# Attention with rotary queries and keys: projecting a query half and a key half in turn instead of all queries and then all keys

## The chip, the cores and the metric

The kernel runs on one core of a Trainium2 chip. A core has TensorE (PE in the profile, with its weight loads shown as PEld), VectorE (DVE), ScalarE (ACT), GpSimd (POOL) and SyncE (SP), each with its own instruction stream; they are ordered only by semaphores. The metric is the device time of one execution in microseconds, lower is better.

## The reference

A transformer block for 32 batch elements ("batches" below) of 256 tokens and 128 channels, all in float32. Only the attention part is touched:

```
h = layernorm(x) * (1 + ca) + sa
q = rope(rmsnorm(einsum('bim,mhd->bhid', h, wq)))      # 8 heads, D = 128
k = rope(rmsnorm(einsum('bim,mhd->bhid', h, wk)))
v = einsum('bim,mhd->bhid', h, wv)
s = q @ k^T / 128, causal mask, softmax
x = x + ga * einsum('bhid,hdm->bim', softmax(s) @ v, wo)
# then a mixture of experts: top 2 of 8, h = layernorm(x) * (1 + cb) + sb
x = x + gb * experts(h)

def _rope(x):   # even, odd are the halves of the last axis
    return concatenate([even * cos - odd * sin, even * sin + odd * cos])
```

## The kernel before

The first part of the kernel is a software pipeline over batches. One body handles, for body number n, the projections of batch n (stage A), the transposes and the value product of batch n-1 (stage B), scores, exponentials and values of batch n-2 (stage C), the residual of batch n-3 (R), the second normalization of n-4 (N2), the routing of n-5 (RT) and the scatter of rows of n-6 (ST). The second part runs the experts and begins when the first has ended; the change doesn't touch it.

Each engine runs the body in eight steps, h = 0 to 7, and each step holds one head of stage C beside one eighth of stage A. The order of the instructions on each engine is the order in which the code is written; there is no scheduler.

**Stage A.** Queries and keys each have TT = 2 token tiles of 128 tokens and H*D = 1024 columns, worked in halves of 512 columns. That gives eight products of 128x512 per batch, four of queries (steps 0 to 3) and four of keys (steps 4 to 7). Product h is written by TensorE (`split_product`, three matmuls, L1225 in the profile) to the PSUM tile `UN[0]` ("unit" in the profile), which has two banks; product h goes to bank h % 2. ScalarE then squares it for the RMS norm (L753), and VectorE rotates it:

- a key half in two operations: `cosines` (L1073) writes product*cos to `roped`, `sines` (L1085) writes the swapped product*sin to `rope_b`; GpSimd adds the two (`add`, L565, semaphore `add_done`).
- a query half (from batch 1 on) in three: `sines` to `rope_b`, `cosines` in place in PSUM, and the sum of both to `roped` (L1120, semaphore `q_added`). In batch 0 the query halves are done like keys.

TensorE may overwrite a bank when VectorE has ended its last read: for a key that is the sines (`rope_done`), for a query the sum (`q_added`). GpSimd scales the finished queries of the batch before by their RMS factors (`scale_queries`, L574), TensorE transposes the tiles of `roped` (L1312) in steps 0, 1 (keys) and 5, 6 (queries), and ScalarE copies them out of the second PSUM tile `UN[1]` (L770).

**Stage C.** In each step TensorE computes the scores of head h, and then the product of values and probabilities of head h-1 (`values_times_probs`, L1249 to L1252, "pv" in the profile). Head 7 has no step after it, so its product follows that of head 6 at once, at the end of step 7. VectorE adds each head's result into `acc`, one step later than the product and in two halves (`add_head`, L1046; L1042 for head 0). The two "pv" buffers alternate, and the code holds product g until head g-2 has been added in full:

```python
def values_times_probs(b, h):
    g = H * b + h
    wait(pe, "exp_done", 2 * (g + 1))
    wait(pe, "acc_done", TT * (g - 1))
```

**Routing.** From body 5 on VectorE also carries small operations of the router, placed by step: among them the maxima (L976, step 5, which wait for GpSimd's `score`, L640), the copy of rows (L1024, steps 4 and 5) and `one_hot` (L985, step 6, just before the first half of `add_head`).

Of the kernel before, what the change touches and what calls it, by code (L numbers as in the profile page):

```python
# [14 lines left out]
ALU = mybir.AluOpType  # L15
# [4 lines left out]
def adaln_block(nc, x, wq, wk, wv, wo, wr, br, w1, b1, w2, b2, c, wmod, rope_cos, rope_sin, out):  # L20
# [40 lines left out]
    with ctx:  # L61
# [246 lines left out]

        PIECE_FROM, HI_AT, LO_AT = 2, 5, 7
# [146 lines left out]
        def _(pool):  # L456
# [50 lines left out]
            def body(half, parity, live):  # L507
# [53 lines left out]
                def add(h):  # L561

                    u, heads = h // 2, slice(h % 2 * HH * D, (h % 2 + 1) * HH * D)
                    wait(pool, "rope_done", 2 * NU * n + h + 1)
                    pool.tensor_tensor(out=roped[parity][:, u, heads], in0=roped[parity][:, u, heads],  # L565
                                       in1=rope_b[:, u % 2, heads], op=ALU.add)\
                        .then_inc(S["add_done" if h >= HH else "q_added"], 1)
# [36 lines left out]
                if n == 0:  # L604
                    add(0)
# [5 lines left out]
                if n == 0:  # L611
                    for h in range(1, HH):
                        add(h)
# [4 lines left out]
                if ST:  # L618
# [5 lines left out]
                                       op=ALU.mult).then_inc(S["place_k_done"], 1)  # L624
                if B:
                    if A:
                        wait(pool, "q_added", HH * n + 3)
                    scale_queries(1)
                if now:
                    scatter(n - 6, parity, 0, 0)  # L630
                if X:
# [4 lines left out]
                        .then_inc(S["h_ready"], 1)  # L636
                if RT:
# [5 lines left out]
                if A:  # L643
                    add(4)
# [9 lines left out]
                if A:  # L654
                    add(5)
# [6 lines left out]
                if A:  # L662
                    add(6)
# [25 lines left out]
        def _(act):  # L689
# [26 lines left out]
            def body(half, parity, live):  # L716
                n = 2 * half + parity
                _, X, A, B, C, R, N2, RT, ST = live
                for h in range(H):
# [24 lines left out]
                    if A:  # L744

                        w, u = 2 * NU * n + h, h // 2
# [4 lines left out]
                        for j in range(HH):  # L751
                            c = HH * (h % 2) + j
                            nc.scalar.activation(squares[:, c * D:(c + 1) * D], UN[0][:, c * D:(c + 1) * D],  # L753
# [85 lines left out]
        def _(dve):  # L839
# [98 lines left out]
            def body(half, parity, live, heads=H):  # L938
# [121 lines left out]
                for h in range(heads):  # L1060
                    w, u, bank = 2 * NU * n + h, h // 2, h % 2
                    t = u % TT
                    heads = slice(bank * HH * D, (bank + 1) * HH * D)
                    in_place = h < HH and n > 0

                    def cosines():
# [3 lines left out]
                        else:  # L1070
                            wait(dve, "tr_done", NU * (n - 1))
                        turned = UN[0][:, heads] if in_place else roped[parity][:, u, heads]
                        nc.vector.tensor_tensor(  # L1073
                            out=turned.rearrange("p (g c) -> p g c", c=D // 2),
                            in0=UN[0][:, heads].rearrange("p (g c) -> p g c", c=D // 2),
# [3 lines left out]
                    def sines():  # L1079

                        if h < HH:
                            wait(dve, "add_done", HH * (n - 1) + h + 1)
                        elif n == 0:
                            wait(dve, "q_added", h - HH + 1)
# [1100 lines left out]
```

## Time and profile before

| | |
|---|---|
| median of 3 runs | 1124.4 us (1123.93 to 1126.92) |
| profiled execution, its own time | 1132.29 us |
| its span, first to last instruction | 1130.5 us |
| busy, share of the span | PE 90%, ACT 85%, DVE 79%, POOL 70% |
| mean granted TensorE clock | 0.965 |

The execution's own time is 1.8 us above its span. A busy share is an average over the attention part (until about 791 us) and the expert part behind it. Times in the rows further down are microseconds from the start of the span. A timeline row gives start, duration, engine, line, operation, tiles with shapes, how often it repeats, and in brackets the idle time ahead of it with what ended it. VectorE's and ScalarE's next instruction can start some 0.1 us before the row of the one before it ends.

### The profile page before, as it was taken

The page shows a single profiled execution, that of the slowest core. Times are in us where ns is not written, and L with a number is a line of the kernel's source. Part 1 is how long each engine was busy: PE and PEld are TensorE (multiplying, and loading weights), DVE is VectorE, ACT ScalarE, POOL GpSimd, SP SyncE. Part 2 cuts the span into 40 slices and gives each one's busy share as a digit, 9 for nine tenths or more (in the row PEclk, how much of TensorE's full clock was granted, in tenths as well). Part 3 has the DMA queues.
Part 4 walks back from the last instruction along what each step waited for, and adds up shares of the span by engine and source line. Part 5 has one row for each costly group of instructions (what it writes and reads, how often), then busy time and mean ns, then how long its engine had stood idle before and what let it go on. Part 6 is the DMA issues. An engine that isn't in the chain of part 4 may idle for free. (4 is left out here: it accounts for less than half of the span.)

```text
span 1130.5 us, 27394 instructions
## 1 busy us (share of the span) xinstructions
PE 1018.9 (90%) x7294; PEld 780.5 (69%) x7294; DVE 896.2 (79%) x2757; ACT 963.0 (85%) x3517; POOL 785.7 (70%) x1197
## 2 busy tenths in 40 slices
PE   5899999999999999999999999999898779989700
PEld 3588888888888888888888888888554434558600
DVE  5788888889998889888888888886768746767647
ACT  6999999999999999999999999997797748888424
POOL 6655578877787877777777777777356675656654
PEclk9999999999999999999999999999999988999955
DMA  5410000100000100000000000000442322320158
GB/s 151 132 34 13 14 17 26 37 25 23 24 23 27 35 15 13 16 16 15 16 16 16 14 16 15 16 15 18 126 112 92 97 77 65 90 68 26 37 188 271
DMA packets 53849, 57.91 MB, mean 51 GB/s; under 512 B 8108, under 2 KB 42783, under 8 KB 53700
## 3 DMA queue, kind: packets, MB, share of 16 engines
q1 hardware_dynamic: 36612, 35.11, 10.5%
q0 software_dynamic: 8640, 16.87, 4.5%
q10 hardware_dynamic: 8448, 4.20, 1.3%
q8 instruction: 63, 1.03, 0.4%
q14 instruction: 86, 0.70, 0.2%
HBM read 33.08 MB, written 23.97 MB: 50 GB/s over the span
## 5 line engine op out<-in xcount | busy, mean ns | idle before, releaser
L753 ACT ACTIVATE squares<-unit 128x128 f32<-128x128 f32 x1024 | 273.3, 303 | 3.6 <-PE unit L1225 3.4
L565 POOL TENSOR_TENSOR roped<-roped,rope_b 128x512 f32<-128x512 f32 x132 | 175.1, 1327 | 91.7 <-DVE rope_b L1085 89.3
L753 ACT ACTIVATION_READ_ACCUMULATOR squares<-unit 128x1 f32 x1024 | 235.2, 236 | 0.0
L1567 POOL DMA_INDIRECT y_rows<-y_out,place_y x142 | 152.2, 1072 | 94.7 <-DVE y_out L1989 49.4
L1085 DVE TENSOR_TENSOR rope_b<-unit,sin_sb 128x512 f32<-128x512 f32 x256 | 174.4, 681 | 14.6 <-ACT squares L753 12.3
L731 ACT ACTIVATE probs<-scores,rr 128x256 f32<-128x256 f32 x256 | 124.3, 485 | 43.5 <-issue 27.4
L1046 DVE SCALAR_TENSOR_TENSOR acc<-pv,den,acc 128x128 f32<-128x128 f32 x448 | 146.2, 341 | 0.3
L1312 PEld LDWEIGHTS unit<-ident_wr,roped 128*128 128x128 f32 x1024 | 117.9, 141 | 31.6 <-ACT k_t L770 13.0
L1312 PE MATMUL unit<-ident_wr,roped 128*128 128x128 f32 x1024 | 135.2, 275 | 1.6 <-POOL roped L565 1.5
L1975 DVE TENSOR_TENSOR hid_lo<-hidden,hid_hi 128x512 f16<-128x512 f32 (+1 forms) x144 | 92.3, 685 | 54.1 <-ACT hid_hi L1675 34.5
L574 POOL TENSOR_TENSOR roped<-roped,rr 128x1024 f32<-128x1024 f32 x64 | 121.5, 1899 | 13.0 <-DVE roped L1120 12.2
L594 POOL DMA_INDIRECT x_rows<-rows,place x108 | 109.1, 1010 | 22.6 <-issue 19.2
L1665 ACT ACTIVATE hidden<-up,b_t 128x512 f32<-128x512 f32 (+1 forms) x184 | 99.0, 598 | 20.3 <-remote 10.6
L1073 DVE TENSOR_TENSOR roped<-unit,cos_sb 128x512 f32<-128x512 f32 x132 | 89.7, 679 | 25.6 <-ACT squares L753 25.2
L1225 PE MATMUL unit<-wqk_hi,h_hi 128*128 128x512 f16 x256 | 97.9, 382 | 7.3 <-DVE rope_b L1085 4.1
L1249 PE MATMUL pv<-vals,probs 128*128 128x129 f32 x512 | 101.1, 279 | 0.1
L1030 DVE RECIPROCAL den<-pv 128x2 f32<-128x2 f32 x256 | 40.6, 159 | 74.1 <-PE pv L1252 74.0
L1267 PE MATMUL scores<-q_t,k_t 128*128 128x128 f32 x512 | 98.9, 275 | 0.5 <-ACT q_t L770 0.5
L1252 PE MATMUL pv<-vals,probs 128*128 128x129 f32 x512 | 99.0, 275 | 0.0
L1269 PE MATMUL scores<-q_t,k_t 128*128 128x128 f32 x512 | 99.0, 275 | 0.0
L1250 PE MATMUL pv<-vals,probs 128*128 128x129 f32 x512 | 99.0, 275 | 0.0
L1270 PE MATMUL scores<-q_t,k_t 128*128 128x128 f32 x512 | 99.0, 275 | 0.0
(304 smaller groups left out, 3061.3 us busy)
## 6 DMA issues: line engine op xcount, KB each, us to landing
shared<-y_rows SPq DMA_DIRECT2D x16, 512.0 KB, 5.6
x_all<-in_L_attn_x SPq DMA_DIRECT2D x32, 128.0 KB, 2.2
h_late<-in_L_ffn_W SPq DMA_DIRECT2D x16, 256.0 KB
out_x<-hidden ACTq DMA_DIRECT2D x16, 256.0 KB, 3.4
rope_b<-x_rows SPq DMA_DIRECT2D x13, 258.0 KB
tile_x<-x_rows SPq DMA_DIRECT2D x12, 258.0 KB
y_rows<-y_out,place_y POOLq DMA_INDIRECT x142
ga_b<-mod_dram SPq DMA_DIRECT2D x32, 64.0 KB
```

The source lines that it names most:

```text
L565: pool.tensor_tensor(out=roped[parity][:, u, heads], in0=roped[parity][:, u, heads], in1=rope_b[:, u % 2, heads], op=ALU.add)\
L574: pool.tensor_tensor(out=v, in0=v, in1=r, op=ALU.mult).then_inc(S["qs_done"], 1)
L594: pool.indirect_dma_start(out=x_rows, out_offset=bass.IndirectOffsetOnAxis(ap=at, axis=0), in_=rows[k][:, j, t, :], in_offset=None).then_i ...
L731: nc.scalar.activation(probs[:, h % NPR, 0:T], SC[h % 2][:, 0:T], ACT.Exp, scale=r[:, kc:kc + 1]).then_inc(S["exp_done"], 1)
L753: nc.scalar.activation(squares[:, c * D:(c + 1) * D], UN[0][:, c * D:(c + 1) * D], ACT.Square, accum_out=ssq[parity][:, u * H + c:u * H + ...
L1046: ins = nc.vector.scalar_tensor_tensor(out=a[:, t, :], in0=o[:, t, 0:M], scalar=den[:, h % 2, t:t + 1], in1=a[:, t, :], op0=ALU.mult, op1= ...
L1085: nc.vector.tensor_tensor(out=rope_b[:, u % 2, heads].rearrange("p (h s c) -> p h s c", h=HH, s=2), in0=UN[0][:, heads].rearrange("p (h s ...
L1249: nc.tensor.matmul(o[:, 0:D + 1], pr[:, 0:P], v[:, 0, h, 0:D + 1], start=True, stop=True)
L1250: nc.tensor.matmul(o[:, VW:VW + D + 1], pr[:, P:2 * P], v[:, 0, h, 0:D + 1], start=True, stop=False)
L1252: nc.tensor.matmul(o[:, VW:VW + D + 1], pr[:, 2 * P:3 * P], v[:, 1, h, 0:D + 1], start=False, stop=True).then_inc(S["o_done"], 1)
L1312: ins = nc.tensor.transpose(UN[1][:, j * P:(j + 1) * P], roped[other][:, u, j * D:(j + 1) * D], ident[:, :])
L1567: pool.indirect_dma_start(out=y_rows, out_offset=bass.IndirectOffsetOnAxis(ap=place_y[i % (2 * SLOTS)][:, s:s + 1], axis=0), in_=y_out[at] ...
```

## The change

`projection(h)` gives each step a new product: kind = h % 2, half = h // 2 % 2, token tile = h // 4. Steps 0, 2, 4 and 6 hold query halves, steps 1, 3, 5 and 7 key halves. All queries now go to bank 0 and all keys to bank 1 of `UN[0]`. Query halves are summed by VectorE in every batch, batch 0 too. GpSimd's four key additions move in its program: `add(1)` behind the offsets, `add(3)` between the two `scale_queries` (its wait for the third `q_added` is gone), `add(5)` and `add(7)` in the places of the old `add(4)` and `add(7)`; the subtraction that makes `h_lo` now comes ahead of the first scatter. The core of the diff:

```diff
+        def projection(h):
+
+            kind, half, t = h % 2, h // 2 % 2, h // HH
+            return kind, half, t, kind * TT + t
...
-                if n == 0:
-                    for h in range(1, HH):
-                        add(h)
+                if A:
+                    add(1)
                 if rest:
                     scatter(n - 7, other, 1, 1)
                 if B:
...
+                if A:
+                    add(3)
                 if B:
-                    if A:
-                        wait(pool, "q_added", HH * n + 3)
                     scale_queries(1)
-                if now:
-                    scatter(n - 6, parity, 0, 0)
                 if X:
...
+                if now:
+                    scatter(n - 6, parity, 0, 0)
                 if RT:
...
                 if A:
-                    add(4)
+                    add(5)
...
                 for h in range(heads):
-                    w, u, bank = 2 * NU * n + h, h // 2, h % 2
-                    t = u % TT
-                    heads = slice(bank * HH * D, (bank + 1) * HH * D)
-                    in_place = h < HH and n > 0
+                    w = 2 * NU * n + h
+                    bank, half_of, t, u = projection(h)
+                    product = UN[0][:, bank * HH * D:(bank + 1) * HH * D]
+                    heads = slice(half_of * HH * D, (half_of + 1) * HH * D)
+                    in_place = h % 2 == 0
...
-                        wait(pe, "rope_done", w - 1)
-                        was, left = (n, h - 2) if h >= 2 else (n - 1, h - 2 + H)
-                        if was > 0 and left < HH:
-                            wait(pe, "q_added", HH * was + left + 1)
+                        if kind:
+                            wait(pe, "rope_done", w - 1)
+                        else:
+                            wait(pe, "q_added", w // 2)
```

VectorE in steps 4 to 6 of a body with routing. Before, all three steps hold keys (cosines L1073, sines L1085); the rows start behind the last `den` of step 3 and run to the end of step 6, with step 5 left out:

```order
L968 TENSOR_REDUCE e_sum<-e_lg 128x2
L1073 TENSOR_TENSOR roped<-unit,cos_sb 128x512
L971 RECIPROCAL e_rec<-e_sum 128x2
L1046 SCALAR_TENSOR_TENSOR acc<-pv,den,acc 128x128
L1024 COPY rows<-pv 128x2x128
L1046 SCALAR_TENSOR_TENSOR acc<-pv,den,acc 128x128
L1085 TENSOR_TENSOR rope_b<-unit,sin_sb 128x512
...
L1073 TENSOR_TENSOR roped<-unit,cos_sb 128x512
L985 TENSOR_TENSOR one_hot<-iota_e,top_i 128x32
L1046 SCALAR_TENSOR_TENSOR acc<-pv,den,acc 128x128 x2
L1085 TENSOR_TENSOR rope_b<-unit,sin_sb 128x512
```

The same place of the changed kernel, where steps 4 and 6 hold queries (L1120 is the sum; most other lines have moved by one or a few numbers):

```order
L967 TENSOR_REDUCE e_sum<-e_lg 128x2
L1085 TENSOR_TENSOR rope_b<-unit,sin_sb 128x512
L970 RECIPROCAL e_rec<-e_sum 128x2
L1045 SCALAR_TENSOR_TENSOR acc<-pv,den,acc 128x128
L1023 COPY rows<-pv 128x2x128
L1073 TENSOR_TENSOR unit<-unit,cos_sb 128x512
L1045 SCALAR_TENSOR_TENSOR acc<-pv,den,acc 128x128
L1120 TENSOR_TENSOR roped<-unit,rope_b 128x512
...
L984 TENSOR_TENSOR one_hot<-iota_e,top_i 128x32
L1045 SCALAR_TENSOR_TENSOR acc<-pv,den,acc 128x128
L1073 TENSOR_TENSOR unit<-unit,cos_sb 128x512
L1045 SCALAR_TENSOR_TENSOR acc<-pv,den,acc 128x128
```

Steps 4 and 6 each hold one 512-column operation more than before (and steps 1 and 3 one less), and in step 6 a 512-column operation now stands between the two halves of `add_head`.

GpSimd from the offsets (L557) to the score of the router (L640), before:

```order
L557 TENSOR_TENSOR off<-mv,rr 128x2 x2
L594 DMA x_rows<-rows,place 69376x129
L574 TENSOR_TENSOR roped<-roped,rr 128x1024
L622 TENSOR_TENSOR place_k<-one_hot,place_e 128x32
L574 TENSOR_TENSOR roped<-roped,rr 128x1024
L594 DMA x_rows<-rows,place 69376x129
L635 TENSOR_TENSOR h_lo<-h_t,h_hi 128x256
L640 TENSOR_TENSOR score<-e_lg,e_rec 128x16
```

and in the changed kernel:

```order
L562 TENSOR_TENSOR off<-mv,rr 128x2 x2
L571 TENSOR_TENSOR roped<-roped,rope_b 128x512
L599 DMA x_rows<-rows,place 69376x129
L579 TENSOR_TENSOR roped<-roped,rr 128x1024
L624 TENSOR_TENSOR place_k<-one_hot,place_e 128x32
L571 TENSOR_TENSOR roped<-roped,rope_b 128x512
L579 TENSOR_TENSOR roped<-roped,rr 128x1024
L635 TENSOR_TENSOR h_lo<-h_t,h_hi 128x256
L599 DMA x_rows<-rows,place 69376x129
L642 TENSOR_TENSOR score<-e_lg,e_rec 128x16
```

Two key additions (L571) have moved ahead of the score, and the scatter and `h_lo` have changed places.

## Rows read from the trace of the kernel before

**Rows 1.** The page: busy time of the engines.
```profile
PE 1018.9 (90%) x7294; PEld 780.5 (69%) x7294; DVE 896.2 (79%) x2757; ACT 963.0 (85%) x3517; POOL 785.7 (70%) x1197
```

**Rows 2.** Busy time in stretches: PE, PEld, DVE, ACT, POOL, clock, DMA.
```profile
16.80:35.10 18.30, 13.22 (x66) 7.44 (x64) 13.75 (x25) 15.51 (x79) 13.71 (x19) 0.91 0.39 110
53.40:76.50 23.10, 23.10 (x175) 18.99 (x175) 18.54 (x50) 21.52 (x94) 13.32 (x19) 1.00 0.25 66
407.40:431.55 24.15, 24.15 (x185) 19.82 (x183) 21.66 (x74) 23.00 (x98) 19.01 (x32) 1.00 0.05 16
407.65:422.80 15.15, 15.15 (x113) 11.89 (x112) 12.71 (x40) 14.91 (x64) 13.01 (x24) 1.00 0.06 17
790.90:815.00 24.10, 19.31 (x148) 15.25 (x146) 15.70 (x77) 16.50 (x37) 9.86 (x21) 1.00 0.43 124
```

**Rows 3.** Timeline of TensorE, one body's products 0, 6, 7 and its last pv.
```profile
407.40 0.38 PE L1225 MATMUL unit<-wqk_hi,h_hi 128*128 128x512 f16 x1
...
425.44 0.38 PE L1225 MATMUL unit<-wqk_hi,h_hi 128*128 128x512 f16 x1
...
428.41 0.38 PE L1225 MATMUL unit<-wqk_hi,h_hi 128*128 128x512 f16 x1
...
429.50 0.39 PE L1250 MATMUL pv<-vals,probs 128*128 128x129 f32 x2
429.73 0.39 PE L1252 MATMUL pv<-vals,probs 128*128 128x129 f32 x2
430.03 0.46 PE L1249 MATMUL pv<-vals,probs 128*128 128x129 f32 x2
...
431.55 0.38 PE L1225 MATMUL unit<-wqk_hi,h_hi 128*128 128x512 f16 x1
```

**Rows 4.** Timeline of VectorE, steps 3 to 6 of the same body.
```profile
421.46 0.69 DVE L1120 TENSOR_TENSOR roped<-unit,rope_b 128x512 f32<-128x512 f32 x1
422.06 0.17 DVE L1030 RECIPROCAL den<-pv 128x2 f32<-128x2 f32 x1
...
422.85 0.69 DVE L1073 TENSOR_TENSOR roped<-unit,cos_sb 128x512 f32<-128x512 f32 x1 [0.56 <-ACT squares L753]
...
424.37 0.68 DVE L1085 TENSOR_TENSOR rope_b<-unit,sin_sb 128x512 f32<-128x512 f32 x1
...
426.01 0.23 DVE L976 MAX8 top_s<-score 128x8 f32<-128x8 f32 x2
...
427.27 0.68 DVE L1085 TENSOR_TENSOR rope_b<-unit,sin_sb 128x512 f32<-128x512 f32 x1
...
428.07 0.68 DVE L1073 TENSOR_TENSOR roped<-unit,cos_sb 128x512 f32<-128x512 f32 x1
428.66 0.70 DVE L985 TENSOR_TENSOR one_hot<-iota_e,top_i 128x32 f32<-128x32 f32 x1
429.29 0.60 DVE L1046 SCALAR_TENSOR_TENSOR acc<-pv,den,acc 128x128 f32<-128x128 f32 x2
```

**Rows 5.** Timeline of ScalarE: the exponentials of head 0 of the next body.
```profile
431.80 0.47 ACT L731 ACTIVATE probs<-scores,rr 128x256 f32<-128x256 f32 x1 [0.91 <-issue]
```

**Rows 6.** Timeline of GpSimd, steps 3 to 6 of the same body.
```profile
419.12 1.90 POOL L574 TENSOR_TENSOR roped<-roped,rr 128x1024 f32<-128x1024 f32 x1
421.17 1.01 POOL L594 DMA_INDIRECT x_rows<-rows,place  x1 [0.15 <-issue]
423.21 0.67 POOL L635 TENSOR_TENSOR h_lo<-h_t,h_hi 128x256 f16<-128x256 f32 x1 [1.03 <-ACT h_hi L760]
423.85 0.20 POOL L640 TENSOR_TENSOR score<-e_lg,e_rec 128x16 f32<-128x16 f32 x1
...
428.03 1.28 POOL L565 TENSOR_TENSOR roped<-roped,rope_b 128x512 f32<-128x512 f32 x1 [0.23 <-DVE rope_b L1085]
```

**Rows 7.** All instructions of the line of one_hot: ns min/median/max, first and last start.
```profile
L985 DVE TENSOR_TENSOR one_hot<-iota_e,top_i x28: 172/694/703, 138.9 to 786.9; 128x32 f32<-128x32 f32 x28
```

More of the change, by code:

```diff
@@ L603, in body @@
                     roots()
-                if n == 0:
-                    add(0)
                 if R:
@@ L751, in body @@
                         for j in range(HH):
-                            c = HH * (h % 2) + j
-                            nc.scalar.activation(squares[:, c * D:(c + 1) * D], UN[0][:, c * D:(c + 1) * D],
+                            c, at = HH * half_of + j, (HH * bank + j) * D
+                            nc.scalar.activation(squares[:, at:at + D], UN[0][:, at:at + D],
                                                  ACT.Square, accum_out=ssq[parity][:, u * H + c:u * H + c + 1])\
@@ L1071, in cosines @@
                             wait(dve, "tr_done", NU * (n - 1))
-                        turned = UN[0][:, heads] if in_place else roped[parity][:, u, heads]
+                        turned = product if in_place else roped[parity][:, u, heads]
                         nc.vector.tensor_tensor(
                             out=turned.rearrange("p (g c) -> p g c", c=D // 2),
-                            in0=UN[0][:, heads].rearrange("p (g c) -> p g c", c=D // 2),
+                            in0=product.rearrange("p (g c) -> p g c", c=D // 2),
                             in1=cos_sb[:, t:t + 1, :].to_broadcast([P, 2 * HH, D // 2]),
@@ L1079, in sines @@
                     def sines():
[L1081 to L1084, printed above, removed]
+                        if in_place:
+                            wait(dve, "add_done", HH * (n - 1) + h // 2 + 1)
+                        else:
+                            wait(dve, "q_added", HH * n + h // 2 + 1)
                         nc.vector.tensor_tensor(
-                            out=rope_b[:, u % 2, heads].rearrange("p (h s c) -> p h s c", h=HH, s=2),
-                            in0=UN[0][:, heads].rearrange("p (h s c) -> p h s c", h=HH, s=2)[:, :, ::-1, :],
+                            out=rope_b[:, t, heads].rearrange("p (h s c) -> p h s c", h=HH, s=2),
+                            in0=product.rearrange("p (h s c) -> p h s c", h=HH, s=2)[:, :, ::-1, :],
                             in1=sin_sb[:, t, :].rearrange("p (o s c) -> p o s c", o=1, s=2)
@@ L1119, in body @@
                         wait(dve, "tr_done", NU * (n - 1))
-                        nc.vector.tensor_tensor(out=roped[parity][:, u, heads], in0=UN[0][:, heads],
-                                                in1=rope_b[:, u % 2, heads], op=ALU.add).then_inc(S["q_added"], 1)
+                        nc.vector.tensor_tensor(out=roped[parity][:, u, heads], in0=product,
+                                                in1=rope_b[:, t, heads], op=ALU.add).then_inc(S["q_added"], 1)
                     elif A:
```

27 lines of the change are left out of this document (12 added, 15 removed).

## The prediction

> **What bounds the kernel now.** The page's busy times [rows 1] name TensorE first, but they mix two parts of the program, so I went to the stretches. One body of the attention part, from its product 0 to that of the next body, lasts 24.15 us [rows 3], and the busy times of that stretch [rows 2] show TensorE busy in all of it, ScalarE 23.00, VectorE 21.66 and GpSimd 19.01 us. So TensorE sets the pace, ScalarE is 1.15 us from doing so, and VectorE 2.5 us.
>
> Busy matmuls overlap, so that alone doesn't show that TensorE never waits. The timeline does: its matmuls start at steady distances of about 0.22 us for a pair of 128x129 passes, 429.50 to 429.73 for one. The next start would be due at 429.95, and it comes at 430.03 [rows 3]. That start is the values product of head 7. It has waited for VectorE: by the code it needs both halves of head 5 added, and that pair of additions runs from 429.29 to 429.89 [rows 4]. From the end of the additions to the matmul are 0.14 us. So the addition of head 5 in step 6 is already on the path, with about nothing to spare; a stall of some 0.08 us per body is there now. What comes late there makes everything late, since TensorE is full and can't catch up.
>
> The Trainium skill bears on that last sentence (Perfetto Trace Analysis, "Identifying the Most-Contended Engine"): matmul busy time is no measure of TensorE's headroom, the weight loads' busy share is a better one. Weight loads are busy 19.82 of the 24.15 us here, and by that rule a body would have up to 4.3 us in which to absorb a stall, so that this change might cost nothing. The timeline speaks against it, since the starts leave no gap; I keep it as one reason behind the rival of no change.
>
> The second view is VectorE's timeline. Step 4 begins when ScalarE has squared product 4: the cosines start at 422.85 after 0.56 us of idle [rows 4]. From there to the additions of head 5 VectorE has no idle time. That is a chain of 7.04 us (422.85 to 429.89) of VectorE alone. What anchors its start is ScalarE: from the exponentials of head 0 to the squares of product 4, 407.65 to 422.80, it is busy 14.91 of 15.15 us [rows 2]. In front of the exponentials of head 0 ScalarE idles 0.91 us, because it waits for TensorE's scores, which come behind that values product [rows 5]. So there is a loop: ScalarE to step 4, VectorE through steps 4 to 6, TensorE's product of head 7 and its scores, and ScalarE again. It takes the 24.15 us of a body.
>
> **The change part by part.**
> A 512-column operation of VectorE takes 0.68 us as a row and 0.60 us from its start to the next one's (421.46 to 422.06, and 428.07 to 428.66 is 0.59) [rows 4]. The change adds none and removes none from body 1 on; it moves the query sum out of steps 1 and 3 into steps 4 and 6.
>
> - *Steps 1 and 3 get 0.60 us shorter each.* Worth nothing: step 4 can't start before the squares of product 4, and VectorE already idles 0.56 us there.
> - *Step 4 gets the sum: +0.60 us* on the chain.
> - *Step 6 is a query step.* Its sines take the place of the cosines, but its own cosines now stand between the two halves of the addition of head 5: +0.60 us ahead of the second half. (Its sum comes behind, and falls on the next waits, which have slack: product 0 of the next body needs it.)
>
> That makes the addition of head 5 end at 429.89 + 1.20 = 431.09, and the values product of head 7 start at 431.23 instead of 430.03: **+1.20 us**.
>
> - *The maxima of step 5.* They need GpSimd's score, which now has two key additions ahead of it. The second, add(3), can't start before the sines of step 3. Step 3 loses its sum, which ended at 421.46 + 0.69 = 422.15 [rows 4], so its last operation, now the sines, ends near 421.55. Then 1.28 (add, rows 6) to 422.91, 1.90 (scaling) to 424.81, 0.64 (h_lo, start to start) to 425.45, the scatter 0.15 + 1.01 to 426.61, and the score 0.20 to 426.83. VectorE would reach the maxima at 426.01 + 0.60 = 426.61 and gets to them near 426.9: **+0.3 us**. If the scatter is quicker to issue or overlaps this is 0; if GpSimd needs 0.2 us more somewhere it is 0.5.
> - *one_hot.* It works on 32 columns and takes 0.694 us in the median, and 0.172 us in its shortest case, the last one [rows 7], at 786.9, where no key addition runs beside it any more. In the body shown it ends with GpSimd's key addition (428.03 + 1.28 = 429.31; 428.66 + 0.70 = 429.36) [rows 4, 6]. The key addition of step 5 still starts just behind the sines of step 5, so I take the same 0.70 us: **+0**. If the two no longer met, the chain would be up to 0.5 us shorter: **-0.5**.
>
> The last point agrees with a rule of the Trainium skill (SBUF — State Buffer, "Who interferes with whom"): an operation of VectorE with both inputs in SBUF contends with a GpSimd instruction that reads SBUF, and one of the two is blocked until the other ends. If that rule held for any pair at any time, each query sum that now runs beside a key addition would be a candidate too; but its first input is in PSUM, so the rule adds nothing for it.
>
> - *Products 6 and 7.* Product 6 needs the sum of step 4. From the first rotation of step 4 to the second are 1.52 us (422.85 to 424.37), then 0.60 and the sum's own 0.68: 425.65; with the latency of 0.14 it is 425.79, against the product's start at 425.44 [rows 3]: 0.35 us late. Product 7 needs the sines of step 5, which ended at 427.27 + 0.68 = 427.95 [rows 4]: 427.95 + 0.60 + 0.3 + 0.14 = 428.99 against 428.41 [rows 3], 0.58 late. Both lie inside the later +1.5 and are not added to it.
> - *GpSimd.* It does four key additions per body as before and has 5.1 us to spare [rows 2]. Behind add(3) in its queue stand the scaling, h_lo, the scatter and the score. The scaling ends at 424.8 by the working above, and the transposes of that tile come behind product 6, so after 426: hidden. h_lo is for the next body. Only the score is waited for in time.
> - *Batch 0 and 1.* VectorE takes four sums of 0.68 from GpSimd in batch 0; VectorE is busy 13.75 of 18.30 us there [rows 2]: within 1 us either way.
>
> **The sum.** 1.2 + 0.3 = 1.5 us per body. It needs routing on VectorE (the small operations and one_hot) together with projections, which is bodies 5 to 31, 27 of them: one_hot runs 28 times [rows 7], the last without projections. In bodies 2 to 4, without routing, VectorE is busy 18.54 of 23.10 us [rows 2]; there the chain is about 1.5 us shorter (one_hot and the small ones) and the extra 1.2 is absorbed. 27 x 1.5 = 40.5; body 31 has less on ScalarE and gives a little back, so **+40 us**. The profiled execution would go from 1132.3 to about 1172; the median of the runs is 7.9 us below that execution, nothing that the change touches explains this, so I add to the median: 1124.4 + 40 = **1164 us**.
>
> **The rivals.**
> 1. *The stall is smaller* (the score comes in time, or one_hot no longer meets a GpSimd addition, or both): 1.2 - 0.5 = 0.7 us per body, (product 7 alone would still be 0.3 late): 27 x 0.3 to 27 x 0.8 = 8 to 22 us, 1132 to 1146.
> 2. *Nothing changes.* TensorE would have to absorb the stall, by starting later work closer together. The spacing speaks against it. 1124.
> 3. *Faster.* Place: the same values product. If the first half's lighter steps let VectorE run ahead, so that head 5 is added before 429.81, the 0.08 us wait there goes, 2.2 us in 27 bodies, and the same lead could give 1 to 3 us in bodies 0 and 1, where TensorE is busy only 13.22 of 18.30 us [rows 2]: 3 to 5 us, 1119 to 1121. It decides itself at the start of step 4: VectorE would have to start it 1.2 us before the squares of product 4 are done, and the trace has it waiting for exactly these.
> 4. *More than that*: GpSimd becomes the bound. Its order now holds scaling behind add(3). If its operations stretch by over 1 us, the score, the query transposes and the values product all slip: 2 to 3 us per body, 1178 to 1205.
> 5. *The clock.* A wait of 1.5 us per 25 could cost TensorE its clock. Where it was busy only 19.31 of 24.10 us the granted clock was 1.00, the 2.4 GHz level [rows 2]; it was 0.91 only in the first stretch. I give it no share of its own.
>
> **How the numbers follow.** The forecast (1.0 to 1.9 us per body, 1151 to 1176) gets 0.72, rival 1 0.12, rival 2 0.04, rival 3 0.06, rival 4 0.06. A measurement here can tell about 0.3%, 3.4 us, from no change. Slower by more: 0.72 + 0.12 + 0.06 = 0.90, less 0.01 for a rival 1 at its edge: 0.89; the same 0.05, faster 0.06. The range of 8 in 10 takes the forecast and the upper end of rival 1, 1144 to 1178.
>
> **What the profile after would show.** Bodies 5 to 31 last about 25.65 us instead of 24.15, bodies 2 to 4 about 23.15 as now. TensorE gets a gap of over 1 us before the values product of head 7, released by VectorE's additions (L1045), and short ones before products 6 and 7. VectorE's steps 4 to 6 run without idle time except before the maxima, where 0.3 us for the score stand. ScalarE's idle time before the exponentials of head 0 grows from 0.9 to about 2.4 us. It would be wrong if bodies last 24.2 us, if the gap lies before products 0 to 5, or if VectorE waits for GpSimd by 1 us or more.

## The result, and the profile after

| | before | changed |
|---|---|---|
| median (lowest to highest) of 4 runs | 1125.66 us (1123.93 to 1128.32) | 1177.39 us (1175.49 to 1178.36) |
| span of the profiled execution | 1130.5 us | 1173.7 us |
| mean granted TensorE clock | 0.965 | 0.966 |

The changed kernel takes 1.0455 times as long (95% interval 1.0428 to 1.0482), 51.7 us more. The two profiled spans differ by only 43.2 us, because the execution profiled before was 6.6 us above the median of before while the one after is 1.9 us below its own. What differs is the expert part behind the attention part, which the change doesn't touch; so the bodies below are the better measure.

The first line of the page after shows that every engine is now busy for a smaller share than in [rows 1]:

```profile
PE 1032.1 (88%) x7294; PEld 781.2 (67%) x7294; DVE 903.2 (77%) x2761; ACT 968.2 (82%) x3517; POOL 777.8 (66%) x1193
```

To see where in the program the time went I measured each body from the logarithm that ScalarE computes at its start to the next one. There are 35, so one per body, up to the end of the attention part. These are distances worked out from the timelines, in us:

| bodies | before | changed | difference, summed |
|---|---|---|---|
| 0 and 1 | 18.26, 18.28 | 21.06, 19.84 | +4.36 |
| 2 to 4 | 23.16, 23.15, 23.37 | 23.38, 23.36, 23.38 | +0.44 |
| 5 to 31 | 24.08, then 24.15, the last 22.80 | 25.26, 25.79, then 26.10 to body 18, 25.71 from 19, the last 23.86 | +46.29 |
| start-up and last bodies | | | -0.02 |
| all | | | +51.07 |

So the loss is where it was forecast, in bodies 5 to 31, but there are two kinds of body, 26.1 and 25.7 us. The windows of one body of each kind stand for the 24.15 us window of [rows 2] (columns: length, then busy time of PE, PEld, DVE, ACT, POOL with their numbers of instructions, granted clock, DMA share and rate):

```profile
408.45:434.56 26.11, 24.59 (x185) 19.82 (x184) 21.84 (x74) 23.21 (x98) 18.96 (x31) 1.00 0.08 24
589.70:615.40 25.70, 24.44 (x184) 19.69 (x183) 20.88 (x73) 22.87 (x97) 18.57 (x31) 1.00 0.05 15
```

VectorE, ScalarE and GpSimd have no more work than before, within some 0.2 us. TensorE has gaps; its row of busy time (24.59 us) overlaps and can hide them. Its timeline of the first of these bodies answers to [rows 3]. It shows products 6 and 7, the end of the values product of head 6, that of head 7, and product 0 of the next body:

```profile
426.77 0.39 PE L1225 MATMUL unit<-wqk_hi,h_hi 128*128 128x512 f16 x1
...
430.44 0.39 PE L1225 MATMUL unit<-wqk_hi,h_hi 128*128 128x512 f16 x1 [0.52 <-DVE rope_b L1085]
...
431.76 0.39 PE L1252 MATMUL pv<-vals,probs 128*128 128x129 f32 x2
433.04 0.46 PE L1249 MATMUL pv<-vals,probs 128*128 128x129 f32 x2 [0.90 <-DVE acc L1045]
...
434.56 0.38 PE L1225 MATMUL unit<-wqk_hi,h_hi 128*128 128x512 f16 x1
```

Product 7 waits 0.52 us for the sines of step 5, and the values product of head 7 waits 0.90 us for the addition of head 5. It was forecast that the gap at the values product would be over 1 us and the one at product 7 short; the loss is spread more evenly over both. VectorE's timeline of the same body, against [rows 4]:

```profile
421.25 0.19 DVE L1013 TENSOR_REDUCE place<-place_k 128x4 int32<-128x32 f32 x1 [0.44 <-POOL place_k L624]
...
422.47 0.68 DVE L1085 TENSOR_TENSOR rope_b<-unit,sin_sb 128x512 f32<-128x512 f32 x1
...
423.92 0.69 DVE L1085 TENSOR_TENSOR rope_b<-unit,sin_sb 128x512 f32<-128x512 f32 x1 [0.62 <-ACT squares L752]
...
426.03 0.68 DVE L1120 TENSOR_TENSOR roped<-unit,rope_b 128x512 f32<-128x512 f32 x1
...
428.43 0.24 DVE L975 MAX8 top_s<-score 128x8 f32<-128x8 f32 x2 [0.67 <-POOL score L642]
...
431.09 0.69 DVE L984 TENSOR_TENSOR one_hot<-iota_e,top_i 128x32 f32<-128x32 f32 x1
431.70 0.34 DVE L1045 SCALAR_TENSOR_TENSOR acc<-pv,den,acc 128x128 f32<-128x128 f32 x1
431.96 0.68 DVE L1073 TENSOR_TENSOR unit<-unit,cos_sb 128x512 f32<-128x512 f32 x1
432.56 0.33 DVE L1045 SCALAR_TENSOR_TENSOR acc<-pv,den,acc 128x128 f32<-128x128 f32 x1
...
435.58 0.67 DVE L1128 SCALAR_TENSOR_TENSOR w_lo<-h_late,w_hi 128x512 f16<-128x512 f32 x1
```

The sum (L1120) of step 4 and the cosines between the halves of head 5's addition stand where the prediction put them. The wait of 0.67 us for the score is more than the 0.3 forecast, and there is a wait that was not forecast at all, 0.44 us for GpSimd's `place_k` in step 3. In bodies from 19 on the first shrinks and the second is gone, but for 0.16 us in body 23:

```profile
635.02 0.24 DVE L975 MAX8 top_s<-score 128x8 f32<-128x8 f32 x2 [0.27 <-POOL score L642]
```

The view of waits over the stretch from 150 to 780 us (total, times, longest) shows that split. VectorE waits for the score in every body of the stretch, 24 times, and for `place_k` 13 times, in bodies 7 to 18 and in body 23:

```profile
PE pv L1249 <- DVE acc L1045: 21.5, 24, 0.9
...
DVE top_s L975 <- POOL score L642: 11.5, 24, 0.7
...
DVE place L1013 <- POOL place_k L624: 5.4, 13, 0.4
```

### The profile page after: what moved, and what is told of

It is laid out like the page before. It is cut to its first block and busy times, and to the rows that moved or that the text cites. A ratio compares the mean times of both kernels' runs of the same rounds, so it can differ in the third digit from the quotient of the medians.

```text
span 1173.7 us, 27269 instructions
## 1 busy us (share of the span) xinstructions
PE 1032.1 (88%) x7294; PEld 781.2 (67%) x7294; DVE 903.2 (77%) x2761; ACT 968.2 (82%) x3517; POOL 777.8 (66%) x1193
## 5 line engine op out<-in xcount | busy, mean ns | idle before, releaser
L571 POOL TENSOR_TENSOR roped<-roped,rope_b 128x512 f32<-128x512 f32 x128 | 169.9, 1327 | 201.4 <-DVE rope_b L1085 201.4
L1085 DVE TENSOR_TENSOR rope_b<-unit,sin_sb 128x512 f32<-128x512 f32 x256 | 174.0, 680 | 42.2 <-ACT squares L752 40.0
L1249 PE MATMUL pv<-vals,probs 128*128 128x129 f32 x512 | 101.4, 280 | 24.3 <-DVE acc L1045 24.1
L1249 PEld LDWEIGHTS pv<-vals,probs 128*128 128x128 f32 x512 | 80.3, 190 | 34.5 <-issue 28.8
L1252 PE MATMUL pv<-vals,probs 128*128 128x129 f32 x512 | 99.0, 275 | 0.0
```

Source lines behind the costliest of these rows:

```text
L1085: nc.vector.tensor_tensor(out=rope_b[:, t, heads].rearrange("p (h s c) -> p h s c", h=HH, s=2), in0=product.rearrange("p (h s c) -> p h s ...
L1249: nc.tensor.matmul(o[:, 0:D + 1], pr[:, 0:P], v[:, 0, h, 0:D + 1], start=True, stop=True)
```

## The experiments

The ten kernels of the experiments ran in three series: a_add_first, a_onehot_late, a_score_early and b_half_late on one chip and a_first_and_score, a_all_three, a_key_first and b_onehot_late on another, on both of which the kernel before takes 1094.7 us, and b_sum0 and a_key_first_onehot on a third, where it takes 1136.5 us. No trace of the kernel before was taken there. The expert part, which none of the edits touches, lasts, counted from the last logarithm, 298.8 us in the trace of b_half_late, 340.1 in that of b_sum0 and 339.6 in that of before, while bodies that an edit doesn't reach are the same everywhere: 24.15 us from body 6 on in b_sum0, and 23.36, 23.37 and 23.39 us for bodies 2 to 4 of a_score_early, within 0.02 of the changed kernel's. So ratios are to the kernel before on the same chip, and kernels are compared by their bodies. The absolute times in the first expectations start from the first result. Here "early" is bodies 7 to 17 and "late" bodies 19 to 30.

| kernel | median, us | ratio (95%) | body early / late, us | attention part, us |
|---|---|---|---|---|
| before | | | 24.15 / 24.15 | 0 |
| changed | 1177.4 | 1.0455 (1.0428 to 1.0482) | 26.11 / 25.71 | +51.1 |
| a_add_first | 1149.5 | 1.0503 (1.0486 to 1.0521) | 26.27 / 25.89 | +56.6 |
| a_onehot_late | 1132.3 | 1.0344 (1.0326 to 1.0361) | 25.64 / 25.25 | +39.1 |
| a_score_early | 1131.2 | 1.0335 (1.0318 to 1.0353) | 25.36 / 25.36 | +37.7 |
| b_half_late | 1110.3 | 1.0147 (1.0130 to 1.0164) | 24.75 / 24.75 | +17.0 |
| a_first_and_score | 1132.2 | 1.0349 (1.0333 to 1.0365) | 25.58 / 25.20 | +39.0 |
| a_all_three | 1118.8 | 1.0224 (1.0208 to 1.0239) | 25.11 / 24.74 | +25.7 |
| a_key_first | 1097.7 | 1.0026 (1.0014 to 1.0038) | 24.24 / 24.24 | +3.8 |
| b_onehot_late | 1090.3 | 0.9965 (0.9951 to 0.9978) | 24.01 / 24.01 | -2.3 |
| b_sum0 | 1141.6 | 1.0027 (0.9984 to 1.0069) | 24.15 / 24.15 | +2.5 |
| a_key_first_onehot | 1140.1 | 1.0041 (1.0007 to 1.0074) | 24.21 / 24.21 | +2.8 |

The last column is the difference to the start of the last logarithm in the trace of before. It is less sharp than the bodies: the stretch ahead of body 0 is up to 0.9 us longer in kernels whose edit doesn't reach it, and body 0 takes 18.74 us in b_half_late and 18.73 in b_onehot_late, which are like the kernel before there, against its 18.26. By its total time alone b_sum0 can't be told from the kernel before, since its interval holds 1.

A second table shows in which step a late body gets longer: the distance from the start of one product to the next (5 to 6 means from product 5 to product 6, 0' and later are the next body), in us. From 2 to 5 and from 0' to 1' all agree within 0.02.

| kernel | 5 to 6 | 6 to 7 | 7 to 0' | 1' to 2' |
|---|---|---|---|---|
| before | 2.97 | 2.96 | 3.14 | 3.28 |
| changed | 3.24 | 3.26 | 4.13 | 3.29 |
| a_add_first | 3.38 | 3.58 | 3.53 | 3.62 |
| a_onehot_late | 3.24 | 3.41 | 3.52 | 3.29 |
| a_score_early | 3.24 | 2.98 | 4.06 | 3.30 |
| b_half_late | 2.97 | 2.97 | 3.73 | 3.30 |
| a_first_and_score | 3.37 | 2.98 | 3.46 | 3.60 |
| a_all_three | 3.38 | 2.98 | 2.98 | 3.62 |
| a_key_first | 2.97 | 3.17 | 3.02 | 3.30 |
| b_onehot_late | 2.97 | 2.97 | 2.98 | 3.30 |
| a_key_first_onehot | 2.97 | 3.17 | 3.00 | 3.29 |

**a_score_early: is the rest the score?** GpSimd computes the score directly behind the second scaling, ahead of `h_lo` and the scatter.

```diff
                     scale_queries(1)
+                if RT:
+                    ... score (moved up, unchanged)
                 if X:
                     ... h_lo
                 if now:
                     scatter(n - 6, parity, 0, 0)
-                if RT:
-                    ... score
```

> The changed kernel, with GpSimd's score directly behind the second scale_queries, ahead of h_lo and the scatter. T: the wait before the maxima of step 5 goes, 0.67 us in the 13 bodies 5 to 17 and 0.3 us in the 14 bodies 18 to 31: 8.7 + 4.2 = 13 us less, 1164; the wait for place_k in step 3 stays and costs nothing, since step 4 waits for ScalarE's squares anyway. R1: product 7 comes earlier by as much, but if only product 6 mattered, 1177. R2: more than 20 us less, below 1157.

Bodies of both kinds take 25.36 us, 1.21 more than before. VectorE's timeline of an early body has no idle time left from step 4 to step 6; its step 4 reads:

```profile
424.54 0.68 DVE L1073 TENSOR_TENSOR unit<-unit,cos_sb 128x512 f32<-128x512 f32 x1
425.13 0.34 DVE L1045 SCALAR_TENSOR_TENSOR acc<-pv,den,acc 128x128 f32<-128x128 f32 x1
425.39 0.68 DVE L1120 TENSOR_TENSOR roped<-unit,rope_b 128x512 f32<-128x512 f32 x1
425.99 0.47 DVE L1161 BATCH_NORM_STATS2 bst<-x_all 128x6 f32<-128x128 f32 x2
```

As expected, some 13 us come back. So 1.21 us is the chain alone, and the wait for the score is the whole rest, 0.75 us in an early and 0.35 in a late body. The wait for `place_k` is still there in the same bodies and costs nothing by itself: step 4 begins with ScalarE's squares anyway.

**a_add_first: the second half of the addition ahead of the cosines.**

```diff
-                    if A and in_place:
-                        cosines()
                     if adds:
                         add_head(*ended, 1)
+                    if A and in_place:
+                        cosines()
```

> The changed kernel, with the second half of add_head ahead of the cosines in query steps. Theory T (the time is lost at the values product of head 7, which waits for a chain of VectorE through steps 4 to 6): the additions of head 5 end 0.60 us earlier in bodies 5 to 31, 27 x 0.6 = 16 us less than the changed kernel's 1177.4, so 1161. Rival R1 (the time is lost where TensorE waits to overwrite a bank, products 6 and 7): these releases don't move or come 0.25 us later, so 1177 or a little more. Rival R2 (GpSimd sets the pace through its score and place_k): 1177.

A miss: it should have given back 0.6 us and is 0.17 us per body longer than the changed kernel. VectorE's timeline of a late body:

```profile
632.36 0.18 DVE L1013 TENSOR_REDUCE place<-place_k 128x4 int32<-128x32 f32 x1 [0.48 <-POOL place_k L624]
...
636.50 0.69 DVE L1073 TENSOR_TENSOR unit<-unit,cos_sb 128x512 f32<-128x512 f32 x1
637.22 0.69 DVE L1120 TENSOR_TENSOR roped<-unit,rope_b 128x512 f32<-128x512 f32 x1
...
639.55 0.24 DVE L975 MAX8 top_s<-score 128x8 f32<-128x8 f32 x2 [0.58 <-POOL score L642]
```

The 0.60 us did come back where they were lost, 4.13 to 3.53 from product 7 to 0' in the table. They were given out again elsewhere: 0.14 before product 6, 0.32 before product 7 and 0.33 in step 1 of the next body, 0.79 in all. Two causes are to be seen in the rows. The waits for GpSimd, 0.48 and 0.58 us, have grown in the late bodies too (the one for the score from 0.27); a chain through GpSimd binds there. And the sum, which needs the result of the cosines just before it, starts 0.72 us behind them instead of 0.60; the addition between them had filled that time.

**a_first_and_score: the same with the score out of the way.** Both edits above together, to see the 0.6 us without GpSimd.

> The changed kernel with both edits: additions of head 5 whole before the cosines, and the score directly behind the second scale_queries. The edit of add_head alone made a body longer by 0.17 us (26.27 and 25.89 against 26.10 and 25.72), the score alone gave 25.36. Theory T2 (two loops of nearly one length: VectorE's chain to the values product of head 7, and one of VectorE and GpSimd through the key additions and the score): with the second cut by the early score, the first gets shorter by 0.60, less 0.12 because the sum of step 4 now follows its cosines directly: bodies of 24.85 to 24.9 us, 13 us below the kernel with the early score alone, 15 to 18 above the kernel before. Rival R3 (the order of the addition's halves never mattered): 25.4 to 25.5.

The 0.60 us do come back where they were lost, 4.06 to 3.46 from product 7 to 0', and are given out again in two other places: 0.13 before product 6 (the 0.12 us between cosines and sum) and 0.30 before the transposes of step 1. TensorE's timeline of one late body has all three waits:

```profile
625.67 0.39 PE L1225 MATMUL unit<-wqk_hi,h_hi 128*128 128x512 f16 x1 [0.23 <-DVE roped L1120]
...
630.59 0.46 PE L1249 MATMUL pv<-vals,probs 128*128 128x129 f32 x2 [0.24 <-DVE acc L1045]
...
635.43 0.74 PE L1312 MATMUL unit<-ident_wr,roped 128*128 128x128 f32 x5 [0.22 <-POOL roped L571]
```

The last one is GpSimd's key addition of step 7, which now starts behind later sines: 1.90 us behind product 0', where it was 1.17 in the changed kernel. In an early body the same wait is longer by 0.38 us, which is all that separates 25.58 from 25.20:

```profile
254.37 1.06 PE L1312 MATMUL unit<-ident_wr,roped 128*128 128x128 f32 x8 [0.59 <-POOL roped L571]
```

So the forecast for this kernel, bodies of 24.85 to 24.9 us, was a miss as well: it had priced the 0.12 and not the wait in step 1.

**a_onehot_late: does one_hot cost 0.5 us for meeting GpSimd?** It is moved from ahead of the additions of step 6 to behind them.

```diff
-                (6, 1): (ONE_HOT,)}
+                (6, 4): (ONE_HOT,)}
```

> The changed kernel, with one_hot moved from before the additions of head 5 to the end of step 6. T: one_hot's slot of 0.61 us (431.09 to 431.70 in the trace) leaves the chain in 27 bodies: 16 us less, 1161. R1: product 7 and product 6 lie ahead of step 6 and don't move, 1177. R2: 1177, or slower, because GpSimd's chosen comes later.

The group of `one_hot` (minimum, median and maximum in ns) in the changed kernel:

```profile
L984 DVE TENSOR_TENSOR one_hot<-iota_e,top_i x28: 170/688/694, 144.3 to 838.0; 128x32 f32<-128x32 f32 x28
```

and in this one:

```profile
L984 DVE TENSOR_TENSOR one_hot<-iota_e,top_i x28: 179/190/194, 146.8 to 826.6; 128x32 f32<-128x32 f32 x28
```

It takes 0.5 us less. That agrees with what the Trainium skill says (SBUF — State Buffer, "Who interferes with whom"): the operation has two inputs in SBUF and is held while a GpSimd instruction reads there.

Bodies get 0.46 us shorter, 12 us in all where 16 were expected. But this doesn't price the meeting alone, because the move takes the whole slot of 0.61 us off the chain. From product 7 to 0' all of it comes back (4.13 to 3.52), and 0.15 is lost again before product 7, since VectorE now waits 0.41 us for the score instead of 0.27. What the meeting costs is better seen in a_key_first below, where `one_hot` stands in its old place without it.

**a_all_three: all three edits at once.**

> The changed kernel with all three edits (additions before the cosines, early score, one_hot at the end of step 6). T2: the values product of head 7 would be due 0.1 us later than in the kernel before; then products 6 and 7, which wait for the sum of step 4 and the sines of step 5, bind: 0.35 to 0.5 us late. Bodies of 24.4 to 24.6 us, 8 to 17 us above the kernel before with the 4 to 5 us that bodies 0 to 4 add. R1 (those bank releases cost nothing): bodies of 24.15, 5 us above.

25.11 and 24.74 us, more than the 24.4 to 24.6 expected. The values product of head 7 no longer waits (2.98 from product 7 to 0'), but 0.41 us before product 6 and 0.34 in step 1 remain. With a full TensorE each of these waits counts in full: 0.41 and 0.34, less the 0.16 that the kernel before loses between product 7 and 0', are the 0.59 us by which a late body is longer than before.

**b_half_late: one half of the term alone, in the kernel before.** In step 6 the second half of the addition stands behind the second rotation of that step.

```diff
-                    if adds:
+                    late_half = h == 6 and A
+                    if adds and not late_half:
                         add_head(*ended, 1)
                     small(h, 3)
...
                     elif A:
                         sines()
+                    if adds and late_half:
+                        add_head(*ended, 1)
```

> The kernel before, with one thing of the changed one: in step 6 the second half of the addition of head 5 comes behind the second rotation. Nothing else moves but that rotation, which comes 0.26 us earlier. T: the values product of head 7 starts 0.6 us later in bodies 5 to 31, 27 x 0.6 = 16 us more than the kernel before, 1141. R1: no change or a gain of up to 1 us, 1125. R2: no change, 1125.

24.75 us, +0.60, all of it from product 7 to 0' (3.14 to 3.73), as expected. One rotation of 0.60 us now stands between the halves, and TensorE's row of the values product shows the wait that it makes (this kernel has three lines more, so its L1252 is the product's first part, L1249 in the kernel before):

```profile
612.44 0.46 PE L1252 MATMUL pv<-vals,probs 128*128 128x129 f32 x2 [0.51 <-DVE acc L1046]
```

**b_onehot_late: the kernel before with one_hot later.** The edit of a_onehot_late.

> The kernel before, with one_hot at the end of step 6. T2: the wait of 0.08 us before the values product of head 7 goes, bodies of 24.05 to 24.10 us, 1 to 3 us less than before. Rival: that wait belongs to something else (the exponentials of head 7), no change; or GpSimd's chosen comes late for TensorE in step 2, slower by 0.2 us per body.

```profile
L985 DVE TENSOR_TENSOR one_hot<-iota_e,top_i x28: 173/182/183, 141.4 to 785.3; 128x32 f32<-128x32 f32 x28
```

24.01 us per body: 0.14 of the 0.5 us can be used, which was all of the stall at head 7's product. Expected were 0.05 to 0.10, from a stall of 0.08 us that the prediction reads off [rows 3]. The missing part stands behind the wait. In the kernel before the pair that has waited is followed by the next one after 0.29 us, not 0.22:

```profile
430.03 0.46 PE L1249 MATMUL pv<-vals,probs 128*128 128x129 f32 x2
430.32 0.39 PE L1250 MATMUL pv<-vals,probs 128*128 128x129 f32 x2
```

and in this kernel the product starts 0.22 us behind the one before it and goes on at that distance:

```profile
429.40 0.39 PE L1252 MATMUL pv<-vals,probs 128*128 128x129 f32 x2
429.62 0.39 PE L1249 MATMUL pv<-vals,probs 128*128 128x129 f32 x2
429.84 0.39 PE L1250 MATMUL pv<-vals,probs 128*128 128x129 f32 x2
```

It is the one version that beats both kernels, 1090.3 against 1094.7 us (0.9965, interval 0.9951 to 0.9978).

**a_key_first: keys in the even steps.** The change with its parity turned round: sums in steps 1, 3, 5 and 7, so that step 4 has none and step 6 has none between the halves. GpSimd adds in the even steps; the rope_b slot of queries is the other one, to keep the buffers free in time.

```diff
-            kind, half, t = h % 2, h // 2 % 2, h // HH
+            kind, half, t = 1 - h % 2, h // 2 % 2, h // HH
...
-                    add(1)
+                    add(0)
...
-                    in_place = h % 2 == 0
+                    in_place = h % 2 == 1
+                    slot = 1 - t if in_place else t
...
```

> The changed kernel with the two kinds exchanged within a pair: keys in steps 0, 2, 4, 6, queries in steps 1, 3, 5, 7, rope_b's places exchanged for the queries, GpSimd's additions of keys 0, 2, 4, 6 in the places of 1, 3, 5, 7. T2: one sum instead of two operations on VectorE's chain (the sum of step 5), and the second GpSimd addition may start a step earlier, so no wait for the score: bodies of 24.75 to 24.85 us, so 16 to 22 us above the kernel before with what bodies 0 to 4 add. R2 (alternating as such is what costs, whatever the order): 25.4 to 25.8, 40 to 50 above.

24.24 us, near the kernel before, and less than forecast. The sum of step 5 is on the chain, but `one_hot` takes

```profile
L984 DVE TENSOR_TENSOR one_hot<-iota_e,top_i x28: 170/178/182, 141.5 to 790.2; 128x32 f32<-128x32 f32 x28
```

because no key addition runs beside it here (GpSimd is idle for 1.5 us up to the end of `one_hot`). +0.6 and -0.5 leave 0.1. The -0.5 was not in the forecast, so that the total came out near the kernel before is in part luck.

**a_key_first_onehot: what are the last 0.1 us?** With one_hot moved behind the additions as well.

> The key-first order with one_hot at the end of step 6. In the key-first run one_hot takes 0.18 us in its old place, and bodies last 24.24 us. T2 says that the 0.1 us above the kernel before is TensorE's wait before product 7, for the sum of step 5, which lies ahead of one_hot: bodies stay at 24.2 to 24.25. Rival: it is still the values product of head 7, then 24.10 to 24.15.

24.21 us: the values product gains nothing more, and product 7 still comes 0.2 us late (3.17 against 2.96). By the code it waits for the sum of step 5. The trace of a_key_first agrees: in a late body the sum's row ends at 601.37 us and product 7 starts at 601.43.

**b_sum0: are the query sums of batch 0 the cost of body 0?** The kernel before with these four sums on VectorE and none on GpSimd.

```diff
-                if n == 0:
-                    add(0)
...
-                if n == 0:
-                    for h in range(1, HH):
-                        add(h)
...
-                    in_place = h < HH and n > 0
+                    in_place = h < HH
...
```

> The kernel before, with batch 0's query halves summed by VectorE as in all other batches (GpSimd's four additions of body 0 left to VectorE), the order of products unchanged. Body 0 of the changed kernel was 2.8 us longer and body 1 1.6 us. T4 (the sums of batch 0 lie on the loop of TensorE's product, ScalarE's squares and VectorE's rotations, because there is nothing else to do in body 0): body 0 2 to 2.8 us longer, body 1 as before, so 2 to 3 us above the kernel before. Rival R4 (the new order of the products costs it): no change.

Body 0 takes 20.53 instead of 18.26 us, body 1 is as before. So the sums alone make 2.27 of the 2.80 us which body 0 of the changed kernel loses, with an uncertainty of about 0.5 us, by which body 0 differs between executions. Body 1 is no sharper in the changed kernel: a_onehot_late and a_score_early, which are like it there, have 19.45 us for its 19.84. In body 0 of the changed kernel TensorE waits for the sums, up to 2.7 us:

```profile
27.26 0.39 PE L1225 MATMUL unit<-wqk_hi,h_hi 128*128 128x512 f16 x1 [2.71 <-DVE roped L1120]
...
31.59 0.58 PE L1225 MATMUL unit<-wqk_hi,h_hi 128*128 128x512 f16 x1 [1.42 <-DVE roped L1120]
```

## Why the prediction was right, and where it was off

The forecast of 1164 us was 13.4 us below the 1177.4 measured. The mechanism was as described, with some terms too small. The result lies 1.4 us above the band that was given 0.72 (1151 to 1176) and 0.6 us inside the upper end of the range, so the size was only just met.

- **+1.20 us on the chain: right, and exact.** a_score_early, with the wait for the score taken out, has 1.21. One half of the term alone, in the kernel before, has 0.60; the other half, the sum in step 4, was not tried by itself and is the difference. It counts in full although VectorE is busy only 21.8 of 26.1 us.
- **+0.3 us for the score: right in kind, mis-sized.** It costs 0.75 in early and 0.35 in late bodies, together 13.8 us (46.3 less the 32.5 of a_score_early), where 27 x 0.3 makes 8.1. Counted from the body's product 0, the score ends at 19.95 us (428.40 less 408.45) where I had 19.43 (426.83 less 407.40). Of GpSimd's rows between, the way from the end of the sines of step 3 to the end of the score has the length forecast, 5.25 against 5.28 us:

```profile
419.10 1.91 POOL L579 TENSOR_TENSOR roped<-roped,rr 128x1024 f32<-128x1024 f32 x1
420.96 0.26 POOL L624 TENSOR_TENSOR place_k<-one_hot,place_e 128x32 f32<-128x32 f32 x1
423.23 1.28 POOL L571 TENSOR_TENSOR roped<-roped,rope_b 128x512 f32<-128x512 f32 x1 [2.01 <-DVE rope_b L1085]
424.46 1.91 POOL L579 TENSOR_TENSOR roped<-roped,rr 128x1024 f32<-128x1024 f32 x1
426.31 0.68 POOL L635 TENSOR_TENSOR h_lo<-h_t,h_hi 128x256 f16<-128x256 f32 x1
427.14 1.00 POOL L599 DMA_INDIRECT x_rows<-rows,place  x1
428.17 0.23 POOL L642 TENSOR_TENSOR score<-e_lg,e_rec 128x16 f32<-128x16 f32 x1
...
435.74 1.66 POOL L571 TENSOR_TENSOR roped<-roped,rope_b 128x512 f32<-128x512 f32 x1 [1.74 <-DVE rope_b L1085]
```

  (The terms of the working add up to 5.18, not 5.28: 421.55 and 1.28 make 422.83 and not 422.91. The 0.08 are about the time by which the addition did start behind the sines, 423.15 to 423.23.) It is these sines that end late, 14.70 us into the body instead of 14.15, because VectorE has waited for `place_k` just before. I had looked at what stands behind `add(3)` in GpSimd's queue, and not at what stands behind `add(1)`: the scaling and `place_k`. `place_k` starts 12.51 us into an early body. The last row explains why early bodies are worse. The key addition of step 7 takes 1.66 instead of 1.28 us beside VectorE's `w_lo` (435.58), and what is behind it in the queue, up to the next body's `place_k`, is later by that. The body that pays is the one behind each `w_lo`, which is why body 18 is still a long one. `w_lo` prepares the experts' weights in bodies 2 to 17, 16 times in all:

```profile
L1128 DVE SCALAR_TENSOR_TENSOR w_lo<-h_late,w_hi x16: 674/674/680, 76.8 to 461.7; 128x512 f16<-128x512 f32 x16
```

  From step 7 of body 18 on the addition takes 1.27 us, and bodies from 19 on are 0.4 us shorter. In these late bodies the sines of step 3 end at 14.29 us and VectorE waits 0.27 us for the score, so there the 0.3 of the forecast was right; what was missed is the early bodies. That the score's way is what makes the two kinds differ is shown by a_score_early, where both are equal. The part of `w_lo` and of `add(1)` in it is read from traces; no run moves them. The kernel before has nearly the same for this addition, 1.65 us up to body 17 and 1.28 from body 18 on, and its `place_k` too comes 0.37 us earlier from body 19 on, where nothing waits for it.
- **one_hot +0: right.** It still took 0.69 us in the median.
- **Products 6 and 7 late but inside the sum: right.** In a late body the distances grow by 0.27 and 0.30, and the one from 7 to 0' by 0.99, together 1.56 (25.71 less 24.15). What products 6 and 7 have waited, the values product of head 7 no longer waits. Product 6 was forecast 0.35 us late: the working took 0.14 us from the end of a 512-column operation to the matmul, where the trace has 0.06 (426.71 to 426.77). Product 7 was forecast 0.58 us late in all, and is 0.57 late in a late body and 0.97 in an early one.
- **GpSimd hidden: half wrong.** Nothing waits for the results of the scaling and of `h_lo`, though both stand ahead of the score; the score and `place_k` are waited for. Rival 4, GpSimd as the bound, has its part in this, though no wait reached the 1 us that was named for it.
- **Batches 0 and 1 within 1 us: wrong, +4.4.** The step that failed took busy time (13.75 of 18.30 us) for slack. In these short bodies TensorE, ScalarE and VectorE hand one bank round in turn, product, squares, rotations, sum, and a sum that has to end before the bank is free lengthens that round. b_sum0 shows 2.27 us of it in body 0. The other 1.56 in body 1 was not tested; that body has sums in steps 4 and 6, and a_key_first, without these, takes 18.39 there. The trace points the same way, with TensorE's longest wait of body 1 at its product 6, which needs the sum of step 4:

```profile
47.74 0.39 PE L1225 MATMUL unit<-wqk_hi,h_hi 128*128 128x512 f16 x1 [2.12 <-DVE roped L1120]
```

- **Bodies 2 to 4 absorbed: nearly.** 0.44 us in all. b_half_late loses as much there, so it comes from the operation between the halves.
- **ScalarE's idle time before the exponentials of head 0** grew from 0.91 to 1.93 us, not 2.4; another 0.61 stands before its squares of product 7, which wait for that product:

```profile
434.81 0.47 ACT L729 ACTIVATE probs<-scores,rr 128x256 f32<-128x256 f32 x1 [1.93 <-issue]
```

- **The clock: right.** The granted clock stayed 1.00, the 2.4 GHz level, in both windows, with TensorE busy 24.59 of 26.11 us in one and 24.44 of 25.70 in the other.

The sum of these: the chain 32.5 (forecast 27 x 1.2 = 32.4), the score 13.8 (8.1), bodies 0 to 4 4.8 (0 to 1), and 51.1 in all for 40 forecast. Of the other 2.3 us of the miss, 1.3 are the median of before, which is higher with a fourth run, 0.7 the difference between medians and traces, and 0.4 the rounding of the forecast. Of the rivals, the smaller stall fell with one_hot still at 0.69 us; "nothing changes" and "faster" fell with the result itself, and with the body of 25.36 us in a_score_early. The rule on the weight loads' busy share (the Trainium skill, Perfetto Trace Analysis, "Identifying the Most-Contended Engine") would have left 4.3 us of room; the trace disagrees: 0.60 us ahead of one matmul cost 0.60 us of the body in b_half_late.

## What to carry to other kernels

In this pipeline, whose fullest engine has no gap, an operation was free or cost its whole length by where it stood between two handovers. So cost a move by the chain from the wait that starts it to the wait that ends it, and not by the engine's busy share. Before pricing a wait for another engine, follow that engine's queue one full period back: its own late start is part of the price. And when a gap is closed, look which wait is next behind it: here 0.60 us won at one place came back as 0.13 and 0.30 at two others.

## What the runs showed of the hardware

- A `one_hot` of 32 columns takes 0.17 to 0.19 us alone and 0.69 us when it starts beside a GpSimd addition of 1.28 us, and it then ends with that addition (429.36 against 429.31 us in the kernel before): VectorE's short operation waits for the long one of GpSimd. In the other direction the GpSimd addition takes 1.66 instead of 1.28 us in the 16 bodies where it runs beside `w_lo`.
- A VectorE operation on 512 columns starts 0.60 us behind the one before, and 0.72 us when it needs that one's result (a_add_first).
- A pair of 128x129 matmuls that has waited costs TensorE some 0.07 us beyond the wait: the next pair starts 0.29 or 0.30 us behind it (430.03 to 430.32 in the kernel before, 612.44 to 612.74 in b_half_late), where 0.22 us is the rule in both traces.
- The kernel before had medians of 1125.7 us with the first result, of 1094.7 us on each of two chips and of 1136.5 us on one more, while the bodies of the attention part from body 2 on that no edit reaches agree within 0.02 us. In the traces the difference lies in the expert part (298.8 us in b_half_late, 340.1 in b_sum0); why is open.
